# Laying a column of scores over the partitions: TensorE transposes in place of f32 products with the unit matrix

## The chip, the cores and the metric

The kernel runs on one core of one Trainium2 chip. The metric is the device time of one execution in microseconds (us), taken as the median of several runs. TensorE does the matrix products, ScalarE (ACT in the profile) and VectorE (DVE) the elementwise work, GpSimd (POOL) and SyncE (SP) small work and most of the DMA issues.

## The reference, cut to what matters

Four graph layers run one after the other on 1250 nodes with 1024 features and 20000 edges; each normalises its input, applies ReLU, computes, and adds to the residual.

- Layer 0 takes `x1 = h @ W1 + b1` (512 features) and then applies four gates. A gate is, per edge, `alpha = tanh(x_i @ gw[:512] + x_j @ gw[512:] + gb)` with `i` the receiver and `j` the sender; each node gets the sum over its edges of `norm * alpha * x_j`.
- Layer 1 is a product with a sparse 1024x1024 matrix, plus a bias. Layer 2 is a graph convolution: a product with W and a sum over neighbours.
- Layer 3 is graph attention: `al = h @ a_l`, `ar = h @ a_r`, `e = exp(-leaky_relu(al[src] + ar[dst]))`, and each node gets the sum of `e * h[dst]` over its edges divided by the sum of `e`, through an ELU.

In both the gates and the attention a score of one node of an edge meets a score of the other node. The kernel treats the graph as a dense matrix of edge counts, so it needs one score along the partitions and the other along the free dimension, the same on every partition.

## The kernel before, in words

The 1250 nodes are padded to 1280, ten tiles (`T`) of 128 rows (`P`); `HT` is five tiles. Every engine runs its own list of instructions in an order written out by hand; semaphores join them. f32 values that go into a product are split into a high and a low part (`_hi`, `_lo`, type fp32r), and a product is three matmuls: hi by hi, hi by lo, lo by hi.

**Gates.** A gate has two halves of receivers (five tiles each), so there are eight halves, `q` 0 to 7. `half_pe(q, r, h)` walks over the ten tiles `s` of senders. For each `s` it does 15 matmuls, five receiver tiles `dd` by three (lines 2482 to 2484), with a block of the mask as the stationary operand and `g_hi` or `g_lo` as the moving one. The mask of a tile `s` is made ahead of it: ACT takes `tanh(U_ALL + v[:, s])` (line 1306), DVE multiplies by the edge counts (line 1841), ACT rounds it to `mask_hi` (line 1311), DVE takes the rest as `mask_lo` (line 1846). The masks lie in a ring of five. DVE reads the finished sums (`take_sums`, line 1856), takes the next scores `u` and `v` by two dot products per tile (`gates`, lines 1716 and 1719), and the low part `g_lo` (line 1724) of what ACT has rounded (`g_hi`, line 1294).

`U_ALL` is 640 columns of PSUM that hold, on every partition, the scores `u` of the five receiver tiles of a half. `spread_u(q, h)` fills it. It waits for the scores (`u_ready`) and until ACT has read the old values for the last time (`tanh_ready`), and does five f32 matmuls whose stationary operand is one column of `u` repeated 128 times (an access pattern of stride 0) and whose moving operand is the unit matrix `ident`. The spread for `q` + 1 is issued in half `q` before tile `s` = 7; the one for `q` = 0 stands in the last tile of the product before the gates (`x1_pe`, `t` = 9, `k` = 2). That makes eight calls, 40 products. ACT's first tanh of a half and one of DVE's `gates` wait for it.

**Attention.** The product of layer 3 is `turned_product(dense[2], ...)`; its matmuls are line 758, and transposes of whole tiles are line 741. DVE takes `al` and `ar` per tile (lines 2150, 2153, 2159). `spread_al` lays `al` over the partitions in the same way, into `TRANSPOSED`: eight tiles (`AL_FIRST`) in the middle of the product of the last tile (`k` = 4), the two others in the first group of the aggregation before `s` = 5. ACT copies the result to `al_all` (lines 1570 and 1554), and ACT and DVE make the attention matrix from it (lines 1519, 2167, 1510, 2171, 1525, 2176); `gat_step` (line 2602) is the aggregation, with the same three matmuls, one group of two receiver tiles after another.

Between the gates and the product of layer 1 lies a chain with transfers: a tile of x is stored, loaded, normalised, its squares are written out (`squares_of_rows`) and read back turned (`turned`), and its parts `hT_hi` (line 652) and `hT_lo` (line 658) feed line 758.

Other places use TensorE's transpose already: line 741 (f32, tiles of the input), line 2346 (f32, rows of weights) and line 2355 (bf16).

Of the kernel before, what the change touches and what calls it, by code (L numbers as in the profile page):

```python
# [24 lines left out]
P = 128  # L25
# [30 lines left out]
HT = T // 2  # L56
# [51 lines left out]
def build_program(nc, x, src, dst, edge_weight, w1, b1, gate_w, gate_b, bias1, w2, b2, w3_dram, att, out):  # L108
# [13 lines left out]
    def small(name, shape, dtype):  # L122
        size = 4 if dtype in (F32, F32R, I32) else 2
        for n in shape[1:]:
            size *= n
        offset = places[0]
        places[0] = -(-(offset + size) // 32) * 32
        assert places[0] <= limit, name
        return at(name, shape, dtype, offset)
# [175 lines left out]
    ident = small("ident", [P, P], F32)  # L305
# [26 lines left out]
    u = small("u", [P, T], F32)  # L332
    v = small("v", [P, T], F32)
    al = small("al", [P, T], F32)
# [196 lines left out]
    TRANSPOSED = ps[:, 6 * BANK:8 * BANK]  # L531
# [16 lines left out]
    U_ALL = ps[:, HT * BANK:HT * BANK + HALF]  # L548
# [1730 lines left out]
    def _(pe):  # L2279
# [88 lines left out]
        def spread_u(q, h):  # L2368


            pe.wait_ge(u_ready, HT * q + HT)
            pe.wait_ge(tanh_ready, 2 * HT * q)
            for dd in range(HT):
                last = nc.tensor.matmul(U_ALL[:, dd * P:(dd + 1) * P], u[:, h * HT + dd:h * HT + dd + 1].to_broadcast([P, P]), ident[:, :],
                                        start=True, stop=True)
            last.then_inc(u_spread, 1)

        def open_bank(b):
# [3 lines left out]
        def x1_pe(t):  # L2382

            b = t % 2
            pe.wait_ge(hT_lo_ready, t + 1)
            if t == 1:
                pe.wait_ge(blend_chain, 3)
                open_bank(1)
            if t + 1 < T and t + 1 != LATE_TILE:
                transpose_pe(pe, d0, (t + 1) // 2, (t + 1) % 2)  # L2390
            for k in range(KT):
                if t + 1 == LATE_TILE and k == KT // 2:
                    transpose_pe(pe, d0, LATE_TILE // 2, LATE_TILE % 2)
                if k % 2 == 0:
                    place_pe(t, k // 2)
                if k == 0:
                    pe.wait_ge(bias_placed, t + 1)
                if t == 1 and k == KT // 2:
                    sum_captured()
                if t == T - 1 and k == 2:  # L2400
                    pe.wait_ge(product_read[0], HT)
                    spread_u(0, 0)
                if t == 0:
                    pe.wait_ge(w_lo_ready, k + 1)
                nc.tensor.matmul(PRODUCT0[b], hT_hi[b][:, k, :], w1_hi[:, k, :], start=False, stop=False, skip_group_check=True)  # L2405
                nc.tensor.matmul(PRODUCT0[b], hT_hi[b][:, k, :], w1_lo[:, k, :], start=False, stop=False, skip_group_check=True)  # L2406
                last = nc.tensor.matmul(PRODUCT0[b], hT_lo[b][:, k, :], w1_hi[:, k, :], start=False, stop=(k == KT - 1), skip_group_check=True)  # L2407
            last.then_inc(product_ready[b], 1)
# [11 lines left out]
        with pe.If(whole == 0):  # L2420
# [4 lines left out]
            with pe.Fori(0, T) as a:  # L2425
# [6 lines left out]
                with pe.Fori(0, GENERAL_CHUNKS) as c:  # L2432
                    n = a * GENERAL_CHUNKS + c
                    pe.wait_ge(gen_ready, n + 1)
                    for q in range(CHUNKS):
                        columns = onehot[q]
                        for lo, hi in BLOCKS:
                            last = nc.tensor.matmul(COUNTS[:, lo:hi], dsel[0:EP, 0, q, :], columns[0:EP, lo:hi], start=False, stop=False, skip_group_check=True)
                        for half, (lo, hi) in zip(WEIGHTS, weight_blocks):
                            for k in range(3):  # L2440
                                last = nc.tensor.matmul(half, dsel[0:EP, 1 + k, q, :], columns[0:EP, lo:hi], start=False, stop=False, skip_group_check=True)
# [3 lines left out]
                for half, (lo, hi) in zip(WEIGHTS, weight_blocks):  # L2445
                    last = nc.tensor.matmul(half, zeros[:, :], iota_h[:, lo:hi], start=False, stop=True, skip_group_check=True)
                last.then_inc(gen_summed, 1)
                pe.wait_ge(gen_copied, 2 * a + 2)
                for s in range(T):
                    last = nc.tensor.transpose(COUNT_T[:, s * P:(s + 1) * P], count_f[:, s * P:(s + 1) * P], ident[:, :])  # L2450
# [12 lines left out]
        def half_pe(q, r, h):  # L2463

            for s in range(T):
                k = s % SLOTS
                if s == HT + 2 and not is_last(q):
                    spread_u(q + 1, 1 - h)
                if s == T - 1 and is_last(q):
                    pe.wait_ge(tanh_ready, 2 * GATES * T)  # L2470
                    transpose_pe(pe, dense[1], 0, 0)
                if h == 0:
                    pe.wait_ge(g_lo_ready, T * r + s + 1)
                pe.wait_ge(mask_lo_ready, 2 * HT * q + s + 1)
                order = LAST_SUMS if is_last(q) and s == T - 1 else range(HT)
                for n, dd in enumerate(order):
                    if is_first(q) and s == 0 and dd == HT - 1:
                        pe.wait_ge(product_read[1], HT)
                    if s == 0 and not is_first(q):
                        pe.wait_ge(sum_read, HT * q - HT + dd + 1)  # L2480
                    cols = slice(dd * P, (dd + 1) * P)
                    nc.tensor.matmul(SUMS[dd], mask_hi[k][:, cols], g_hi[:, s, :], start=(s == 0), stop=False)  # L2482
                    nc.tensor.matmul(SUMS[dd], mask_hi[k][:, cols], g_lo[:, s, :], start=False, stop=False)  # L2483
                    last = nc.tensor.matmul(SUMS[dd], mask_lo[k][:, cols], g_hi[:, s, :], start=False, stop=(s == T - 1))  # L2484
                    if s == T - 1 and n < HT - 1:
                        last.then_inc(sum_ready, 1)
                last.then_inc(mask_used, 1)
# [98 lines left out]
        def spread_al(tiles):  # L2586

            pe.wait_ge(al_copied, tiles[-1] + 1)
            for t in tiles:
                last = nc.tensor.matmul(TRANSPOSED[:, (t - tiles[0]) * P:(t - tiles[0] + 1) * P],  # L2590
                                        al[:, t:t + 1].to_broadcast([P, P]), ident[:, :], start=True, stop=True)
            last.then_inc(al_spread, 1)

        turned_product(dense[2], lambda b: pe.wait_ge(unit_read, (UNIT_OF["S4", 3] + 1, UNIT_OF["A22", 2] + 1)[b]), lambda: spread_al(range(AL_FIRST)))

        def gat_step(s, j, ns):
# [10 lines left out]
        def quarter_step(s, q):  # L2607

            cols = slice(P, 2 * P)
            of = slice(HID + q * QUARTER, HID + (q + 1) * QUARTER)  # L2610
            for left, rights in ((att_hi[s][:, cols], (y_hi[s], y_lo[s])), (att_lo[s][:, cols], (y_hi[s],))):
                for right in rights:
                    last = nc.tensor.matmul(LAST_QUARTERS[q], left, right[:, of], start=(s == 0 and len(rights) == 2 and right is y_hi[s]),
                                            stop=(s == T - 1 and len(rights) == 1))
            return last
# [5 lines left out]
        def gat_pe(grp, first):  # L2621

            for s in range(T):
                if first:
                    pe.wait_ge(product_read[s % 2], dense[2].pairs(s // 2 + 1))
                    if s == HT:
                        pe.wait_ge(al_all_ready, 1)
                        spread_al(range(AL_FIRST, T))
                pe.wait_ge(att_lo_ready, T * grp + s + 1)
                for j in range(GRP):  # L2630
                    if s == 0 and not first:
                        pe.wait_ge(gat_read, GRP * grp - GRP + j + 1)
                    last = gat_step(s, j, range(2))
                    if j == GRP - 1:
                        last.then_inc(att_used, 1)
                    if s == T - 1:
                        row_sums(j).then_inc(gat_ready, 1)
# [18 lines left out]
        for q in range(2):  # L2656
            for s in range(T):
                last = quarter_step(s, q)
# [24 lines left out]
```

## Time and profile before

| | before |
|---|---|
| median of 3 runs | 967.32 us (967.18 to 970.75) |
| the profiled execution, its own time | 967.41 us |
| its span, first to last instruction | 965.6 us |
| TensorE busy | 943.4 us, 98% |
| VectorE, ScalarE, GpSimd busy | 705.7, 495.2, 154.4 us |
| mean granted TensorE clock | 0.996 |

PE is TensorE's matmuls and PEld its loads of the stationary operand, which run beside them. Starts of instructions are measured; the ends of matmuls are modelled, so the cost of a matmul in a dense stream is read from one start to the next, not from its duration. "Idle before" with a name behind an arrow is the time for which an engine waited, and for what.

### The profile page before, as it was taken

The numbers are of one execution on the slowest core, as the hardware profiler recorded it, in microseconds if no ns is written. First come the engines' busy times: TensorE is split into PE (matmuls) and PEld (weight loads), VectorE is DVE, ScalarE is ACT, GpSimd is POOL, SyncE is SP. The second block draws the span as 40 slices with busy tenths as digits, with TensorE's granted clock in tenths as the row PEclk, the third lists the DMA queues.
The fourth block names the chain that finished last, engine by engine and source line by source line (L and its number), as shares of the span: only waits on it lengthen the run. The fifth ranks groups of instructions, "written<-read, shape, count | busy, mean of one in ns | idle before, by whom it ended". The sixth has DMA issues, their size and how long they took to land.

```text
span 965.6 us, 13857 instructions
## 1 busy us (share of the span) xinstructions
PE 943.4 (98%) x5011; PEld 783.1 (81%) x5012; DVE 705.7 (73%) x1243; ACT 495.2 (51%) x759; POOL 154.4 (16%) x247
## 2 busy tenths in 40 slices
PE   5999999999999999979999999999999999999998
PEld 3888878888888888868888888888888888888887
DVE  7887797797788788638763244598757875967787
ACT  5788874554554557324433453443623223656654
POOL 3023410000000001213342000013320000333331
PEclk9999999999999999999999999999999999999999
DMA  7256492000000005299982400042986532201222
GB/s 260 89 195 232 118 205 85 0 23 1 0 22 0 0 0 119 48 286 295 315 241 109 161 1 2 1 55 89 229 192 210 170 113 82 88 25 62 88 87 82
DMA packets 41433, 105.75 MB, mean 110 GB/s; under 512 B 6136, under 2 KB 14524, under 8 KB 41232
## 3 DMA queue, kind: packets, MB, share of 16 engines
q1 hardware_dynamic: 29056, 70.27, 21.6%
q0 software_dynamic: 12320, 34.74, 15.8%
q8 instruction: 34, 0.56, 0.3%
q14 instruction: 23, 0.19, 0.1%
HBM read 63.03 MB, written 47.20 MB: 114 GB/s over the span
## 4 chain that ended last, share of the span: by engine, by line
PE 90%; DVE 4%; DMA 3%; ACT 2%; issue 1%; POOL 1%; SPq 0%; DVEq 0%; ACTq 0%; POOLq 0%
PE ps L758 21%; PE ps L2602 14%; PE ps L2577 10%; PE ps L2482 9%; PE ps L2484 8%; PE ps L2483 8%; PE ps L2550 5%; PE ps L2546 5%; PE ps L2405 2%; PE ps L2407 2%; PE ps L2406 2%; PE ps L741 1%; DMA squares_of_rows<-squares 1%; DVE wt_lo L588 1%; PE ps L2330 1%; PE ps L2333 1%
## 5 line engine op out<-in xcount | busy, mean ns | idle before, releaser
L2482 PE MATMUL ps<-g_hi,mask_hi 128*128 128x512 f32 x400 | 157.6, 394 | 0.2 <-DVE mask_lo L1846 0.2
L2484 PE MATMUL ps<-g_hi,mask_lo 128*128 128x512 f32 x400 | 155.9, 390 | 0.0
L2483 PE MATMUL ps<-g_lo,mask_hi 128*128 128x512 f32 x400 | 155.8, 389 | 0.0
L1306 ACT ACTIVATE mask<-ps,v 128x640 f32<-128x640 f32 x80 | 63.1, 793 | 95.7 <-PE ps L2484 49.1
L2602 PE MATMUL ps<-y_all,att_hi 128*128 128x512 f32 x380 | 103.6, 392 | 0.0
L2482 PEld LDWEIGHTS ps<-g_hi,mask_hi 128*128 128x128 f32 x400 | 75.1, 188 | 19.1 <-DVE mask_lo L1846 2.3
L2484 PEld LDWEIGHTS ps<-g_hi,mask_lo 128*128 128x128 f32 x400 | 75.1, 188 | 15.9
L2483 PEld LDWEIGHTS ps<-g_lo,mask_hi 128*128 128x128 f32 x400 | 75.1, 188 | 14.9
L2577 PE MATMUL ps<-w_hi,parts 128*128 128x512 f32 x280 | 86.5, 389 | 0.0
L758 PE MATMUL ps<-w,hT_hi 128*128 128x512 f32 x320 | 85.8, 390 | 0.0
L2602 PEld LDWEIGHTS ps<-y_all,att_hi 128*128 128x128 f32 x380 | 70.4, 188 | 14.8 <-issue 0.4
L717 ACT ACTIVATE xin<-xin,shift 128x1024 f32<-128x1024 f32 x30 | 34.4, 1148 | 81.0 <-DVE shift L600 81.0
L1841 DVE TENSOR_TENSOR mask<-mask,countT 128x640 f32<-128x640 f32 x80 | 65.4, 819 | 14.0 <-ACT mask L1306 13.9
L1311 ACT ACTIVATE mask_hi<-mask 128x640 fp32r<-128x640 f32 x80 | 59.0, 737 | 28.4 <-DVE mask L1841 27.9
L758 PE MATMUL ps<-wt_hi,hT_hi 128*128 128x512 f32 x160 | 63.6, 397 | 6.6 <-DVE hT_lo L658 6.6
L758 PEld LDWEIGHTS ps<-w,hT_hi 128*128 128x128 f32 x320 | 59.8, 188 | 12.5
L1846 DVE TENSOR_TENSOR mask_lo<-mask,mask_hi 128x640 fp32r<-128x640 f32 x80 | 65.1, 818 | 1.2 <-ACT mask_hi L1311 1.2
L2550 PE MATMUL ps<-cnt,hs 128*128 128x512 f32 (+1 forms) x240 | 64.8, 351 | 0.0
L2546 PE MATMUL ps<-cnt,hs 128*128 128x512 f32 (+1 forms) x240 | 64.6, 351 | 0.0
L758 PE MATMUL ps<-wt_lo,hT_hi 128*128 128x512 f32 x160 | 63.1, 394 | 0.0
L2577 PEld LDWEIGHTS ps<-w_hi,parts 128*128 128x128 f32 x280 | 52.6, 188 | 10.8
L2602 PE MATMUL ps<-y_all,att_lo 128*128 128x512 f32 x190 | 59.4, 390 | 0.0
(255 smaller groups left out, 1952.3 us busy)
## 6 DMA issues: line engine op xcount, KB each, us to landing
xin<-x_after SPq DMA_DIRECT2D x20, 512.0 KB, 5.4
squares_of_rows<-squares SPq DMA_DIRECT2D x16, 512.0 KB, 4.1
turned<-squares_of_rows SPq DMA_DIRECT2D x64, 128.0 KB, 2.9
x_after<-g POOLq DMA_DIRECT2D x20, 256.0 KB, 7.6
x_after<-row_all POOLq DMA_DIRECT2D x10, 512.0 KB, 8.4
xres<-x_after POOLq DMA_DIRECT2D x10, 512.0 KB, 5.7
x_after<-xres POOLq DMA_DIRECT2D x10, 512.0 KB, 4.7
xin<-in_x SPq DMA_DIRECT2D x9, 512.0 KB, 3.7
```

What stands on the lines that cost most here:

```text
L758: last = nc.tensor.matmul(PRODUCT[d.n][b][:, half * BANK:(half + 1) * BANK], left[:, k, :], right[k][:, half * BANK:(half + 1) * BANK], st ...
L1306: nc.scalar.activation(mask[k][:, :], U_ALL, ACT.Tanh, bias=v[:, s:s + 1]).then_inc(tanh_ready, 1)
L1311: nc.scalar.activation(mask_hi[k][:, :], mask[k][:, :], ACT.Copy).then_inc(mask_hi_ready, 1)
L1841: nc.vector.tensor_tensor(mask[k][:, :], mask[k][:, :], countT[:, s, h * HALF:(h + 1) * HALF], ALU.mult).then_inc(mask_ready, 1)
L1846: nc.vector.tensor_tensor(mask_lo[k][:, :], mask[k][:, :], mask_hi[k][:, :].bitcast(F32), ALU.subtract).then_inc(mask_lo_ready, 1)
L2482: nc.tensor.matmul(SUMS[dd], mask_hi[k][:, cols], g_hi[:, s, :], start=(s == 0), stop=False)
L2483: nc.tensor.matmul(SUMS[dd], mask_hi[k][:, cols], g_lo[:, s, :], start=False, stop=False)
L2484: last = nc.tensor.matmul(SUMS[dd], mask_lo[k][:, cols], g_hi[:, s, :], start=False, stop=(s == T - 1))
L2546: nc.tensor.matmul(sums[j], hs[:, f, s, 0, j * P:(j + 1) * P], columns, start=(s == 0), stop=False)
L2550: last = nc.tensor.matmul(sums[j], hs[:, f, s, 1, j * P:(j + 1) * P], columns, start=False, stop=(s == T - 1))
L2577: last = nc.tensor.matmul(UNIT_BANK[n], left, right[:, k, :], start=(kind != "A22" and k == 0 and len(rights) == 2 and right is W2_HI[w]), ...
L2602: last = nc.tensor.matmul(AGG[j][:, n * BANK:(n + 1) * BANK], left, right[:, n * BANK:(n + 1) * BANK], start=(s == 0 and len(rights) == 2 ...
```

## The change

The products of `spread_u` and `spread_al` become transposes of the same operand, the stride-0 column, against the same `ident`. The destination, the order, the waits and the semaphores stay as they are; no other line is touched.

```diff
             for dd in range(HT):
-                last = nc.tensor.matmul(U_ALL[:, dd * P:(dd + 1) * P], u[:, h * HT + dd:h * HT + dd + 1].to_broadcast([P, P]), ident[:, :],
-                                        start=True, stop=True)
+                last = nc.tensor.transpose(U_ALL[:, dd * P:(dd + 1) * P], u[:, h * HT + dd:h * HT + dd + 1].to_broadcast([P, P]), ident[:, :])
             last.then_inc(u_spread, 1)
...
             for t in tiles:
-                last = nc.tensor.matmul(TRANSPOSED[:, (t - tiles[0]) * P:(t - tiles[0] + 1) * P],
-                                        al[:, t:t + 1].to_broadcast([P, P]), ident[:, :], start=True, stop=True)
+                last = nc.tensor.transpose(TRANSPOSED[:, (t - tiles[0]) * P:(t - tiles[0] + 1) * P],
+                                           al[:, t:t + 1].to_broadcast([P, P]), ident[:, :])
             last.then_inc(al_spread, 1)
```

## Rows read from the trace of the kernel before

**Rows 1.** The page: busy time and share; the chain's shares; one DMA (us to landing).

```profile
PE 943.4 (98%) x5011; PEld 783.1 (81%) x5012; DVE 705.7 (73%) x1243; ACT 495.2 (51%) x759; POOL 154.4 (16%) x247
...
PE 90%; DVE 4%; DMA 3%; ACT 2%; issue 1%; POOL 1%; SPq 0%; DVEq 0%; ACTq 0%; POOLq 0%
...
squares_of_rows<-squares SPq DMA_DIRECT2D x16, 512.0 KB, 4.1
```

**Rows 2.** Waits of PE: us in total, times, longest us.

```profile
PE ps L758 <- DVE hT_lo L658: 6.6, 1, 6.6
...
PE ps L2482 <- DVE mask_lo L1846: 0.2, 1, 0.2
```

**Rows 3.** The lines asked for: duration ns min/median/max, first and last start.

```profile
L2374 PEld LDWEIGHTS ps<-ident,u x80: 187/190/192, 116.5 to 359.3; 128*128 128x128 f32 x80
L2374 PE MATMUL ps<-ident,u x80: 271/275/275, 116.7 to 359.4; 128*128 128x128 f32 x80
...
L741 PEld LDWEIGHTS ps<-ident,xin x112: 138/140/231, 7.7 to 716.7; 128*128 128x128 f32 x112
L741 PE MATMUL ps<-ident,xin x112: 270/273/476, 7.7 to 716.8; 128*128 128x128 f32 x112
```

**Rows 4.** PE in order of time: start us, us, instruction; five products in a gate.

```profile
146.61 1.28 PE L2374 MATMUL ps<-ident,u 128*128 128x128 f32 x10
147.65 0.47 PE L2482 MATMUL ps<-g_hi,mask_hi 128*128 128x512 f32 x1
```

**Rows 5.** The same view: eight products, then two, in layer 3.

```profile
814.88 1.95 PE L2590 MATMUL ps<-ident,al 128*128 128x128 f32 x16
816.58 1.17 PE L758 MATMUL ps<-w,hT_hi 128*128 128x512 f32 x4
...
836.04 0.61 PE L2590 MATMUL ps<-ident,al 128*128 128x128 f32 x4
836.40 1.18 PE L2602 MATMUL ps<-y_all,att_hi 128*128 128x512 f32 x4
```

**Rows 6.** The same view: eight transposes inside the last half, and eight of weights.

```profile
400.96 1.03 PE L741 MATMUL ps<-ident,xin 128*128 128x128 f32 x8
401.75 0.48 PE L2482 MATMUL ps<-g_hi,mask_hi 128*128 128x512 f32 x1
...
84.03 1.03 PE L741 MATMUL ps<-ident,xin 128*128 128x128 f32 x8
84.90 0.20 PE L2330 MATMUL ps<-right,left 125*128 125x90 bf16 x1
```

**Rows 7.** ACT, DVE and PE in order of time, first tiles of half 0.

```profile
118.03 0.80 ACT L1306 ACTIVATE mask<-ps,v 128x640 f32<-128x640 f32 x1 [0.16 <-PE ps L2374]
...
128.11 0.82 DVE L1846 TENSOR_TENSOR mask_lo<-mask,mask_hi 128x640 fp32r<-128x640 f32 x1
...
131.65 0.81 DVE L1846 TENSOR_TENSOR mask_lo<-mask,mask_hi 128x640 fp32r<-128x640 f32 x1
...
128.53 0.39 PE L2484 MATMUL ps<-g_hi,mask_lo 128*128 128x512 f32 x1
129.08 0.47 PE L2482 MATMUL ps<-g_hi,mask_hi 128*128 128x512 f32 x1 [0.15 <-DVE mask_lo L1846]
```

**Rows 8.** ACT, DVE and PE in order of time, end of half 1.

```profile
183.18 0.79 ACT L1306 ACTIVATE mask<-ps,v 128x640 f32<-128x640 f32 x1 [4.31 <-PE ps L2374]
...
184.62 0.75 DVE L1724 SCALAR_TENSOR_TENSOR g_lo<-g,dis,g_hi 128x512 fp32r<-128x512 f32 x1 [5.79 <-ACT g_hi L1294]
...
191.09 3.38 DVE L1856 SCALAR_TENSOR_TENSOR g<-ps,dis,g 128x512 f32<-128x512 f32 x5
...
182.81 0.47 PE L2482 MATMUL ps<-g_hi,mask_hi 128*128 128x512 f32 x1
...
193.16 0.39 PE L2482 MATMUL ps<-g_hi,mask_hi 128*128 128x512 f32 x1
```

**Rows 9.** Busy us (instructions) of PE, PEld, DVE, ACT, POOL, clock, DMA share, GB/s.

```profile
182.00:217.00 35.00, 35.00 (x160) 28.68 (x159) 31.03 (x54) 19.87 (x28) 0.00 (x0) 1.00 0.04 16
362.00:405.00 43.00, 42.95 (x193) 35.06 (x192) 32.20 (x45) 24.74 (x31) 5.29 (x6) 1.00 0.33 80
```

**Rows 10.** The chain that ended last, between the gates and layer 1's second tile.

```profile
408.56 1.21 DVE stats L596 x2
...
412.79 11.03 DMA squares_of_rows<-squares
...
425.20 7.20 DMA turned<-squares_of_rows
...
434.87 1.21 PE ps L758 x2
```

**Rows 11.** As rows 9: the clock before, in and after TensorE's longest pause.

```profile
400.00:410.00 10.00, 10.00 (x49) 8.09 (x49) 6.53 (x14) 2.51 (x3) 5.30 (x7) 1.00 0.69 110
430.00:435.00 5.00, 0.13 (x1) 0.14 (x1) 1.49 (x2) 2.09 (x2) 0.00 (x0) 0.73 1.07 361
435.00:440.00 5.00, 5.00 (x14) 3.96 (x15) 3.60 (x6) 1.15 (x1) 0.57 (x1) 0.59 1.06 253
```

**Rows 12.** ACT, DVE and PE in order of time after the spread of `al`.

```profile
816.86 1.03 ACT L1570 ACTIVATE al_all<-ps 128x1024 f32<-128x1024 f32 x1 [4.59 <-PE ps L2590]
...
829.92 0.42 DVE L2176 TENSOR_TENSOR att_lo<-att_e,att_hi 128x256 fp32r<-128x256 f32 x1
...
833.16 0.41 DVE L2176 TENSOR_TENSOR att_lo<-att_e,att_hi 128x256 fp32r<-128x256 f32 x1
...
830.48 1.16 PE L2602 MATMUL ps<-y_all,att_hi 128*128 128x512 f32 x4
```

## The prediction

> **What bounds the kernel now.** I read the page first: TensorE is busy for 943.4 of 965.6 us and carries 90% of the chain that ended last, VectorE 4%, DMA 3% [rows 1]. So a microsecond taken out of TensorE's stream is worth a microsecond, unless something else is waiting just behind it. PE's waits show where that is: 6.6 us in one piece for `hT_lo` of layer 1, and 0.2 us for one `mask_lo`; in between PE does not stand still [rows 2]. Then I looked at the changed lines themselves, and read neighbouring starts from the timeline, because ends of matmuls are modelled: the cost of a spread is the time from its first start to the start of what follows.
>
> **What the change removes and adds.** The 40 products of `spread_u` leave 80 records, so an f32 product is two of them; a transpose on line 741 leaves one (112 records are 14 calls of eight) [rows 3]. The durations, 275 and 273 ns, are alike and say nothing; starts do. Ten records of product take 147.65 - 146.61 = 1.04 us [rows 4], sixteen take 1.70, four take 0.36 [rows 5]: a slope of (1.70 - 0.36) / 12 = 0.112 us a record and an offset of -0.09. Eight transposes in the same surroundings, a dense stream of 512-column matmuls, take 401.75 - 400.96 = 0.79 us [rows 6]; the line for products gives 8 x 0.112 - 0.09 = 0.81 for eight records. So a transpose costs what half an f32 product costs, and I price it as one record:
>
> - five instead of ten records: 1.04 - (0.56 - 0.09) = 0.57 us for a call of `spread_u`;
> - eight in place of sixteen: 1.70 - 0.79 = 0.91 us;
> - two in place of four: 2 x 0.112 = 0.22 us.
>
> From the other side: eight transposes before narrow bf16 matmuls took 0.87 us, 0.109 each [rows 6]. At that price with no offset the savings are 0.50, 0.83 and 0.14.
>
> What the trace does not show is a transpose of a stride-0 column. The row that is nearest says the repetition is free in a plain load: the stationary load of `u` takes 190 ns. The load of a transpose takes 140 ns at full stride [rows 3]. I take 140, or anything that stays hidden. Bounds: the longest transpose of the trace, 476 ns [rows 3], which would make a transpose dearer than the two records it replaces; and no cost beyond the 0.10 us of its start to start.
>
> A rule of the Trainium skill differs from the row. "TensorE: Matmul & The Clock Gate", section Terms, says that transpose mode is four times faster for FP32. The trace shows a factor of 0.224 / 0.10, about two, and the sum goes by the trace; by that rule a spread of five would take 1.12 / 4 = 0.28 us and the kernel would come out near 960 us (it returns as a rival below).
>
> **Which savings reach the end.** Taking the ten calls in order of time:
>
> - *The first `spread_u`, before half 0: nothing.* PE starts the third tile of half 0 at 129.08, 0.55 us after the start before it where 0.23 is usual, because `mask_lo` ran from 128.11 to 128.93 [rows 7]. In those first tiles DVE has two mask passes, one `g_lo` and two dot products per tile: 131.65 - 128.11 = 3.54 us from one `mask_lo` to the next [rows 7], to PE's 15 matmuls at (193.16 - 182.81) / 45 = 0.23 [rows 8], 3.45. DVE and ACT got there by a chain that starts in the edge counts and the tables, and that does not pass through the spread except for one tanh that had waited 0.16 us [rows 7]. PE will finish the spread 0.57 us earlier and wait that much longer for the mask. If I am wrong the kernel gains 0.57 more.
> - *The seven others: 7 x 0.57 = 4.0 us.* PE does not wait at all from there to the last half. The danger is that DVE is nearly as busy: 31.0 of 35 us in half 1 [rows 9]. But DVE's late part of that half is released by the spread itself: ACT waited 4.31 us for line 2374, its first tanh started at 183.18, its `g_hi` followed, and DVE, which had stood idle for 5.79 us, went on at 184.62 and reached the sums at 191.09 [rows 8]. PE's first matmul of the next half, which needs the first of those sums read, starts at 193.16, 2 us after that. A spread that ends 0.57 us earlier moves ACT and DVE forward by the same 0.57. The shorter half still leaves DVE 34.4 - 31.0 = 3.4 us.
> - *The pause between gates and layer 1 neither gives nor takes.* Its chain starts behind the gates: DVE's statistics at 408.56, a store of squares that takes 11.03 us, their way back 7.20 us [rows 10]. The DMA engines are full there but were a third full from 362 to 405 [rows 9], so the queue is made by work that follows PE, and moves with it.
> - *The spreads of `al`: 0.91 + 0.22 = 1.1 us.* ACT waited 4.59 us for the first, then 13 us of attention work on ACT and DVE lead to the `att_lo` that ends at 830.34 and lets PE start at 830.48 [rows 12]. Natural would have been about 830.3, so the two chains are level here. Both of them start at the end of the spread, so both come 0.91 us earlier. At the second PE has slack: the `att_lo` of the tile that follows it started at 833.16 and PE took it up at 836.40 [rows 5, 12].
>
> No DMA, wait or semaphore is added or moved; SP's and POOL's queues keep their order. PE gets 50 records and 50 loads fewer.
>
> **The sum.** 4.0 + 0.9 + 0.2 = 5.2 us with roundings (7 x 0.575 = 4.03, 0.91, 0.22). The profiled execution took 967.41 us around its span of 965.6, and lies 0.1 above the median of the three. 967.4 - 5.2 = 962.2 us, a gain of 0.53%. The bounds: 7 x 0.50 + 0.83 + 0.14 = 4.5 us by the dearer transpose, 5.2 + 0.57 = 5.8 with the first spread counted. One more thing moves the result: in the pause the granted clock fell to 0.5, the 1.2 GHz level, for about 1.35 / 0.5 = 2.7 us of 430 to 435 and 4.1 us of 435 to 440 [rows 11]; PE worked again from 434.87 [rows 10] and the clock rose at about 439.1, so (439.1 - 434.87) / 2 = 2.1 us are lost. In another execution that could be nothing, or all 6.8 us could fall on work and cost 3.4. So the forecast's own range is 960.4 to 963.8.
>
> **The rivals.**
>
> - *Transposes as forecast: 962.2 us. 0.70.*
> - *The change does nothing on TensorE:* for a repeated column the transpose costs the same 0.22 us as a product, two passes under another name. For it: no row shows this operand in a transpose. Against: line 741 has one record where a product has two [rows 3]. 967.4 us. 0.07.
> - *Half of it is eaten by the pause:* the transfers behind 412.79 run on a clock of their own, PE reaches the pause 4.0 us sooner and waits 10.6 instead of 6.6. For it: an 11 us store where the page's median is 4.1 [rows 1, 10], so the engines are contended. Against: the low share before 405 [rows 9]. Only the spreads of `al` remain: 967.4 - 1.1 = 966.3 us. 0.08.
> - *Transposes at a quarter of a product:* the saving per transpose would be 0.224 - 0.056 = 0.17 us, times 45 (7 x 5 + 8 + 2) 7.6 us: 959.8 us. Against: 0.79 us for eight [rows 6]. The rule of the Trainium skill named above says this. 0.06.
> - *The other side, a slow load:* the stationary load of a repeated column in transpose form reads one address 128 times and blocks PE. At 0.224 us a transpose nothing is won, and at 0.224 + 4.84 / 45 = 0.33 us the kernel is 0.5% slower; at the 0.476 us of the longest transpose [rows 3] it loses 45 x 0.25 = 11 us: 979 us. Against: 190 ns for the plain load of this column, no more than any other f32 load. 0.04.
> - *The clock falls:* transposes do not hold the full clock, and every run of five brings a fall like that in the pause, worth up to 3.4 us [rows 11]; two falls outweigh the gain, nine calls would cost 30 us: some 990 us. Against: 400 to 410, with eight transposes in it, has clock 1.00 [rows 11]. "TensorE: Matmul & The Clock Gate", section Part 4: PE-mode transpose, of the Trainium skill says that transposes do not count as busy for the clock; by that rule this would be likelier than I make it. 0.03.
> - Something else: 0.02.
>
> **How the numbers follow.** The time is that of the likeliest, 962.2 us. From 959.8 to 966.6 the range takes in nearly all of the forecast's own (0.65), the quarter price and the pause: 0.79, about 8 in 10; no change and the slow cases lie above it. About 0.5%, or 4.84 us, is what a measurement of this kernel can tell from no change: that is 962.48, and my forecast lies just beyond it. Of the forecast's 0.70 I give 0.41 to faster; with the quarter price and a little of the rest faster is 0.49. Within 0.5% are 0.29 of the forecast, no change, the pause and a little of the slow cases: 0.46. Slower 0.05.
>
> **What the profile after would show.** Line 2374 and its twin should have 40 and 10 records in place of 80 and 20, with a load near 140 ns. The start after a spread of five should follow at about 0.47 us, after eight at 0.79. The wait for `mask_lo` at the third tile of half 0 should grow by about half a us. The last half should begin 4.0 us sooner, the wait for `hT_lo` should stay near 6.6, and the end of the spread of `al` should be 4.9 us sooner. If the spacing is 0.22 the product was never the cost; if the wait for `hT_lo` has grown the pause took it. The prediction fails by little if the clock falls for another stretch than before, and by much only if a repeated column loads slowly.

## The result and the profile after

The changed kernel takes 960.43 us in the median of five runs (959.77 to 962.06), the kernel before 967.32 (967.17 to 970.75). The ratio is 0.9929, with a 95% interval of 0.9916 to 0.9943. The forecast was 962.2 us, a gain of 5.2; measured are 6.9. The profiled execution took 961.20 us with a span of 959.5.

The spreads in the profile after: duration ns min/median/max for the first line of the group, then PE in order of time.

```profile
L2374 PEld LDWEIGHTS ps<-ident,u x40: 134/136/137, 115.2 to 354.0; 128*128 128x128 f32 x40
L2374 PE MATMUL ps<-ident,u x40: 271/272/273, 115.4 to 354.1; 128*128 128x128 f32 x40
...
115.42 0.71 PE L2374 MATMUL ps<-ident,u 128*128 128x128 f32 x5
...
179.90 0.71 PE L2374 MATMUL ps<-ident,u 128*128 128x128 f32 x5
180.37 0.48 PE L2481 MATMUL ps<-g_hi,mask_hi 128*128 128x512 f32 x1
...
809.88 1.03 PE L2589 MATMUL ps<-ident,al 128*128 128x128 f32 x8
810.67 1.17 PE L758 MATMUL ps<-w,hT_hi 128*128 128x512 f32 x4
...
830.10 0.38 PE L2589 MATMUL ps<-ident,al 128*128 128x128 f32 x2
830.24 1.17 PE L2601 MATMUL ps<-y_all,att_hi 128*128 128x512 f32 x4
```

Half of the records are left, and from one start to the next a spread takes 0.47 us where it took 1.04 [rows 4], 0.79 for 1.70 and 0.14 for 0.36 [rows 5]. The durations of a record, 272 for 275 ns, still say nothing. The load of the repeated column takes 136 ns, no more than the 140 of a column that is not repeated [rows 3].

The waits of PE and the places where it starts after one:

```profile
PE ps L758 <- DVE hT_lo L658: 7.5, 1, 7.5
...
PE ps L2295 <- POOL ew_part L1011: 1.3, 1, 1.3
PE ps L2481 <- DVE mask_lo L1846: 0.4, 1, 0.4
...
119.86 0.39 PE L2406 MATMUL ps<-w_hi,hT_lo 128*128 128x512 f32 x1
120.33 0.47 PE L2481 MATMUL ps<-g_hi,mask_hi 128*128 128x512 f32 x1
...
127.78 0.47 PE L2481 MATMUL ps<-g_hi,mask_hi 128*128 128x512 f32 x1 [0.39 <-DVE mask_lo L1846]
...
422.36 0.61 PE L758 MATMUL ps<-wt_hi,hT_lo 128*128 128x512 f32 x2
430.43 0.79 PE L758 MATMUL ps<-wt_hi,hT_hi 128*128 128x512 f32 x1 [7.46 <-DVE hT_lo L658]
```

With landmarks in both profiles the 6.1 us between the two spans can be laid out. The kernel before has its last start ahead of the pause at 427.69; the other numbers stand in the rows here, in [rows 4, 5, 7, 10] and in the two spans.

| stretch | before | after | difference |
|---|---|---|---|
| start of the program to the first spread | 116.72 | 115.42 | -1.30 |
| first spread to the third tile of half 0 | 12.36 | 12.36 | 0.00 |
| third tile to the last start ahead of the pause | 298.61 | 294.58 | -4.03 |
| over the pause | 7.18 | 8.07 | +0.89 |
| end of the pause to the spread of `al` | 380.01 | 379.45 | -0.56 |
| spread of `al` to the end | 150.72 | 149.62 | -1.10 |

Three rows are the change: 0.00, 4.03 and 1.10. Three are not in its code: the start, the pause, and the stretch behind the pause, where PE runs at half speed for a while, about 3 us here and about 4 before. The second row of the change can be seen in each half. PE from one spread to the next, first the kernel before (its earlier spread is in [rows 4]), then the changed one:

```profile
181.77 1.28 PE L2374 MATMUL ps<-ident,u 128*128 128x128 f32 x10
```

```profile
145.32 0.71 PE L2374 MATMUL ps<-ident,u 128*128 128x128 f32 x5
```

That is 181.77 - 146.61 = 35.16 us before and 179.90 - 145.32 = 34.58 after, 0.58 less; the halves that follow save 0.57 to 0.61 each. ACT, DVE and the next half follow the spread as they did before:

```profile
180.74 0.80 ACT L1306 ACTIVATE mask<-ps,v 128x640 f32<-128x640 f32 x1 [3.74 <-PE ps L2374]
...
182.18 0.75 DVE L1724 SCALAR_TENSOR_TENSOR g_lo<-g,dis,g_hi 128x512 fp32r<-128x512 f32 x1 [5.22 <-ACT g_hi L1294]
...
188.64 2.06 DVE L1856 SCALAR_TENSOR_TENSOR g<-ps,dis,g 128x512 f32<-128x512 f32 x3
...
190.69 0.39 PE L2481 MATMUL ps<-g_hi,mask_hi 128*128 128x512 f32 x1
```

DVE's first sum stands 2.05 us ahead of PE's start of the next half, 2.07 before [rows 8]: the spread carries DVE with it. ACT and DVE waited 0.57 us less each.

### The profile page after: what moved, and what is told of

Same layout as the page of the kernel before. It is cut to its first block, busy times and chain, and to the rows that moved or that the text cites. A ratio compares the mean times of both kernels' runs of the same rounds, so it can differ in the third digit from the quotient of the medians.

```text
span 959.5 us, 13757 instructions
## 1 busy us (share of the span) xinstructions
PE 936.8 (98%) x4961; PEld 776.0 (81%) x4962; DVE 705.5 (74%) x1243; ACT 494.9 (52%) x759; POOL 155.4 (16%) x247
## 4 chain that ended last, share of the span: by engine, by line
PE 89%; DVE 5%; DMA 3%; ACT 2%; issue 1%; SPq 0%; DVEq 0%; ACTq 0%
PE ps L758 21%; PE ps L2601 14%; PE ps L2576 10%; PE ps L2481 9%; PE ps L2483 8%; PE ps L2482 8%; PE ps L2549 5%; PE ps L2545 5%; PE ps L2404 1%; DMA xin<-in_x 1%; PE ps L2406 1%; PE ps L2405 1%; DMA squares_of_rows<-squares 1%; PE ps L741 1%; DVE wt_lo L588 1%; PE ps L2330 1%
```

## The experiments

The theory to be tested: the gain is the number of TensorE records times 0.112 us, the first spread excepted. Rivals: the pause eats a part; the change makes the start of the program faster, or wins in some way that is not the number of records. "Gain" is the difference of medians on the same chip; the ratio goes with its interval.

**Only the spreads of u.** The edit is the first hunk of the diff alone.

> Only the spreads of u are transposes; the spreads of al stay f32 products. Price theory (a record is worth 0.112 us, the first spread nothing): 7 x 0.57 = 4.0 us faster, ratio 0.9958. Rival, the pause between gates and layer 1 eats what comes before it: under 1 us faster, and the wait for hT_lo near 10.6 us. Rival, the change shortens the start of the program as well (the changed kernel reached the first spread 1.3 us sooner): 5.3 us faster and the first spread near 115.4 us.

963.74 us, ratio 0.9961 (0.9947 to 0.9976), a gain of 3.4 us by the medians and 3.8 by the ratio, near the price theory's 4.0. The wait for `hT_lo` was 6.1 us, not 10.6, and the first spread started at 117.86, 1.1 us later than in the kernel before. Both rivals fail here.

**Only the spreads of al.** The second hunk alone.

> Only the spreads of al are transposes. Price theory: 1.1 us faster, ratio 0.9988, all of it behind 814 us. Rival, a saving of 1 us here is lost because the attention chain on ACT and DVE is level with PE: no difference, and a longer wait for att_lo at the fourth tile. Rival of the start: 2.4 us faster.

965.88 us, ratio 0.9985 (0.9976 to 0.9995): 1.2 to 1.5 us for the 1.1 expected. From the spread (815.03) to the end of the span (964.7) it is 149.67 us, as in the changed kernel.

**The kernel before, once more,** without an edit.

> The kernel before, unchanged. All theories: ratio 1.000. It shows how far the profiled start of the program differs from execution to execution: if the 1.3 us by which the changed kernel reached its first spread sooner is chance, this profile can have its first spread anywhere from about 115 to 117 us; if it belongs to the change, at 116.7.

966.93 us, ratio 0.9996 (0.9987 to 1.0005). Its profile has the first spread at 115.07, so the 1.3 us at the start are chance. In the profiles of this study that start lay between 115.07 and 117.86 us, whatever the kernel. Two things vary there. One is how long PE waits for `ew_part` behind the first loads, 0.6 to 3.6 us. The other is how long PE then still runs at half speed, 0.43 us from start to start: to 22.57 us in the first profile of the kernel before, and only to about 19.9 in this one. Both had waited 2.0 us for `ew_part`, and yet their first spreads are 1.65 us apart.

The stretches of the table tell the change from chance. The three rows of the change add up to 461.69 us in the first profile of the kernel before and to 461.74 in this one. In the changed kernel they are 456.56 us, and 456.57 in its second profile (below). That is 5.1 to 5.2 us both times. The three other rows add up to anything from 502.8 to 505.1 us in the eleven profiles without a filled pause, with transposes or with products.

**Every transpose twice.**

```diff
-            for dd in range(HT):
+            for dd in [dd for _ in range(2) for dd in range(HT)]:
...
-            for t in tiles:
+            for t in [t for _ in range(2) for t in tiles]:
```

> Every transpose of both spreads is issued twice, so that PE makes as many records as before the change. Price theory (a transpose costs what half an f32 product costs): ratio to before 1.000, within 0.5 us, starts after a spread of ten 1.04 us later. Rival, the change wins in another way than by the number of records (start, or ACT getting the scores earlier): still 1 us or more faster than before. Each record of a transpose being dearer than one of a product, 0.120 against 0.112: 0.4 us slower.

966.88 us, ratio 0.9993 (0.9983 to 1.0003). With as many records as before the gain is gone, within the interval. PE in order of time in this kernel:

```profile
181.36 1.25 PE L2374 MATMUL ps<-ident,u 128*128 128x128 f32 x10
182.37 0.48 PE L2481 MATMUL ps<-g_hi,mask_hi 128*128 128x512 f32 x1
```

Ten transposes take 1.01 us, ten records of product 1.04 [rows 4]: a transpose is a little cheaper than half a product, not dearer. Nothing else of the change shows a weight of its own.

**The changed kernel again.**

> The changed kernel once more, beside others on one chip. Price theory, now with only_u at 0.9961 and only_al at 0.9985: the parts add up to 5.2 us, ratio 0.9946. The first comparison gave 0.9929 (6.9 us); if a part of that belongs to the change as a whole and to neither part alone, it comes again: ratio 0.993.

961.12 us, ratio 0.9938 (0.9925 to 0.9951), a gain of 6.3 us by the medians. The sum of the parts, 0.9946, lies inside the interval, and so does the first comparison's 0.9929. The wait for `hT_lo` was 6.5 us this time.

**All but the first spread.**

```diff
             for dd in range(HT):
-                last = nc.tensor.transpose(U_ALL[:, dd * P:(dd + 1) * P], ...)
+                if isinstance(q, int) and q == 0:
+                    last = nc.tensor.matmul(U_ALL[:, dd * P:(dd + 1) * P], ..., start=True, stop=True)
+                else:
+                    last = nc.tensor.transpose(U_ALL[:, dd * P:(dd + 1) * P], ...)
```

> As the changed kernel, but the spread before half 0 stays a product. Theory that the first spread is worth nothing since PE waits for the mask anyhow: the same time as the changed kernel, and a wait for mask_lo at the third tile back at 0.15 us (a step from start to start of 0.55 in place of 0.78). Rival, every spread is worth its 0.57 us: 0.6 us slower than the changed kernel.

963.15 us, ratio 0.9951 (0.9939 to 0.9964). The medians are 2 us apart and the intervals overlap, so the time alone can't settle half a microsecond. The profile can. In order of time, PE:

```profile
116.88 1.28 PE L2375 MATMUL ps<-ident,u 128*128 128x128 f32 x10
...
128.69 0.39 PE L2487 MATMUL ps<-g_hi,mask_lo 128*128 128x512 f32 x1
129.24 0.47 PE L2485 MATMUL ps<-g_hi,mask_hi 128*128 128x512 f32 x1 [0.16 <-DVE mask_lo L1846]
```

From the first spread to the third tile it is 129.24 - 116.88 = 12.36 us, the same as in the changed kernel (127.78 - 115.42) and in the kernel before (129.08 - 116.72, [rows 7] and the table above). The wait stands at 0.16 with the product and at 0.39 with the transpose. The first spread is worth nothing up to there.

**Every product twice.** The same loops as above, in the kernel before.

> The kernel before, with every product of both spreads issued twice: 80 and 20 more records. Price theory: 7 x 10 x 0.112 + 20 x 0.112 = 10.1 us slower, and up to 1.1 more for the first spread, since its wait covers at most 0.57 us or so of the 1.12: 10.1 to 11.2 us, ratio 1.0105 to 1.0115. Rival, PE has slack and absorbs it, or ACT and DVE fall behind for lack of scores: clearly less, or more than 12 us.

977.81 us, ratio 1.0102 (1.0088 to 1.0117): 10.4 us slower by the medians, 9.9 by the ratio. Behind the spread of `al` (824.54) it is 977.5 - 824.54 = 152.96 us, 2.24 more than before, which is 20 x 0.112. From the first spread (116.56) to the third tile (130.01) it is 13.45 us, 1.09 more: making the first spread longer costs nearly all of its 1.12, though making it shorter gains nothing. ACT's first tanh then waits 1.28 us for the spread, where it had waited 0.16 [rows 7], and the mask comes late with it. From the third tile to the pause it is 7.89 us more. By the stretches the cost is thus 7.89 + 2.24 + 1.09 = 11.2 us, where the medians say 10.4; the interval, 8.5 to 11.3 us, holds both.

**A transpose at full stride.**

```diff
-                last = nc.tensor.transpose(U_ALL[:, dd * P:(dd + 1) * P], u[:, h * HT + dd:h * HT + dd + 1].to_broadcast([P, P]), ident[:, :])
+                last = nc.tensor.transpose(U_ALL[:, dd * P:(dd + 1) * P], ident[:, :], ident[:, :])
```

> As the changed kernel, but the spread of u transposes the unit matrix itself, 128 columns side by side, in place of one column repeated: the gates then get other scores and the output is not the reference's. If the repetition of the column costs or saves nothing: the same time as the changed kernel, five transposes 0.46 to 0.47 us, the load 138 to 140 ns in place of 136. If it slows the load: this kernel is faster than the changed one.

962.13 us, ratio 0.9942 (0.9928 to 0.9956), as the changed kernel. The load, in ns:

```profile
L2374 PEld LDWEIGHTS ps<-ident x40: 138/140/143, 115.6 to 354.4; 128*128 128x128 f32 x40
```

140 against 136: repeating a column costs nothing, the load even takes 4 ns less.

**The pause filled, in the changed kernel and in the one before.** The clock behind the pause was the one place left where a microsecond could hide, so I took the fall of the clock away.

```diff
             free(1)
+            if d.n == 1:
+                for _ in range(24):
+                    nc.tensor.matmul(PRODUCT[1][1][:, 0:BANK], zeros[:, :], zeros[:, 0:1].to_broadcast([P, BANK]), start=True, stop=True, skip_group_check=True)
             product_pe(pe, d, 0, 1, False, None)
```

> The changed kernel with 24 products of zeros, 512 columns each, put into TensorE's pause before the second tile of layer 1 (24 x 0.227 = 5.4 us of a pause of 7 to 8; their bank is overwritten by the product that follows). The step from one start to the next after the pause showed half speed for 3 to 5.5 us in each profile, 1.5 to 3 us lost. If the clock then stays at full speed: 1.5 to 3 us faster than the changed kernel, near 959 us, ratio to before 0.991. Rival, the products of zeros do not hold the clock, or the chain of transfers behind the pause gets longer: the same time as the changed kernel or slower.

> The kernel before with the same 24 products of zeros in the pause. It tells whether the 1 us by which the change beat the sum of its parts (6.0 to 6.9 against 5.2 us) lies in the clock after the pause. If it does: this kernel is 2.1 to 3 us faster than before, ratio 0.9975, and the distance to the changed kernel with the pause filled is 5.2 us. If the extra belongs elsewhere the distance is 6 us or more.

The changed kernel with it: 960.24 us, ratio 0.9926 (0.9910 to 0.9942). The kernel before with it: 965.02 us, ratio 0.9985 (0.9973 to 0.9996), a gain of 2.0 us. Busy us, clock (third from the end), DMA share and GB/s, first of the changed kernel, then of the changed kernel with the pause filled:

```profile
425.00:430.00 5.00, 0.00 (x0) 0.00 (x0) 0.93 (x1) 2.02 (x2) 0.00 (x0) 0.67 1.06 355
430.00:435.00 5.00, 4.57 (x14) 3.67 (x15) 3.60 (x7) 1.22 (x2) 0.57 (x1) 0.65 0.98 249
```

```profile
425.00:430.00 5.00, 4.66 (x21) 3.53 (x19) 0.05 (x1) 1.06 (x2) 0.04 (x1) 1.00 1.06 341
430.00:435.00 5.00, 3.61 (x16) 3.00 (x17) 3.57 (x6) 2.19 (x2) 0.57 (x1) 1.00 1.04 262
```

Products of zeros hold the clock at its 2.4 GHz level. In the kernel before that is worth 2.0 us by the medians and 1.5 by the ratio, for the 2.1 us which the prediction had read as lost. The two profiles agree: from the end of the pause to the spread of `al` it is 378.03 us with the pause filled, 380.01 without. The two filled kernels are 4.8 us apart by their medians, and 0.9926 / 0.9985 = 0.9941 gives 5.7: on either side of 5.2. The pair shows no gain of 6 us or more, but with intervals of 1 to 1.5 us each it can't place a missing one either.

**The changed kernel a third time.**

> The changed kernel a third time. Sum of the parts: ratio 0.9946. If the first two comparisons (0.9929 and 0.9938) were not chance: 0.993 to 0.994 again.

961.87 us, ratio 0.9945 (0.9927 to 0.9962): the sum of the parts. The profiled execution was an odd one of 967.81 us. It shows something that I had not looked for. DVE, then PE, in order of time:

```profile
156.83 0.15 DVE L1865 COPY gb_col<-gb 128x1 f32 x1 [5.86 <-DMA gw<-in_L_gnn_gate_w]
...
158.46 3.38 DVE L1856 SCALAR_TENSOR_TENSOR g<-ps,dis,g 128x512 f32<-128x512 f32 x5
...
156.33 0.39 PE L2483 MATMUL ps<-g_hi,mask_lo 128*128 128x512 f32 x1
159.26 0.50 PE L2481 MATMUL ps<-g_hi,mask_hi 128*128 128x512 f32 x1 [2.54 <-DVE g L1856]
...
161.12 0.63 PE L2482 MATMUL ps<-g_lo,mask_hi 128*128 128x512 f32 x1
161.55 0.63 PE L2483 MATMUL ps<-g_hi,mask_lo 128*128 128x512 f32 x1
```

The weights of the second gate (`gw`, 512 KB) are loaded while the DMA engines are full (a busy share of 0.83 to 1.22 from 138 to 150 us in this profile); in this execution the transfer took 18.37 us in the chain that ended last, and 12.7 in the first profile of the changed kernel. DVE waits for it at the head of half 1, ahead of two mask passes and the sums for which PE waits next. PE stood for 2.54 us and then, from 161.1 to 164.1, ran at half speed, 0.43 us from start to start, with a granted clock of 0.50. From its second spread to its third it is 39.03 us in place of 34.58: 4.45 us of the 6.7 by which this span is longer than that of the profile before it (966.1 for 959.4). Another 2.1 us lie behind the pause, with a wait of 0.87 us at line 2549 for which the profile names no cause.

The filled kernel's profile has the same event in a smaller form: a transfer of 16.3 us, a wait of 3.79 us on DVE, then 0.47 us of PE for `g` and 0.37 for `mask_lo`, and 36.05 us from the second spread to the third. That is 1.47 us more than usual, with the clock at 1.00 behind the waits.

**DVE's wait moved to the first use of gw.** On top of the filled pause:

```diff
             if nxt is not None:
-                dve.wait_ge(gw_landed, 16 * (nxt + 1))
                 if h == 1:
...
                     if s == 1:
+                        dve.wait_ge(gw_landed, 16 * (nxt + 1))
                         dve.wait_ge(sum_read, HT * q)
```

> The changed kernel with the pause filled, and with DVE's wait for the gate's weights (gw) moved from the head of half 1 to its first use, behind two mask passes and the five sums. In the profiles so far DVE stood in that wait for 0.5 to 5.9 us at the head of half 1, and in the longest case PE then waited 2.5 us for the sums and ran at half speed behind that. If this is what the late wait costs: no PE wait for g or mask_lo near 158 us in the profile even when gw lands late, a median as in the filled kernel (960.2) or up to 0.5 us below, and no execution several us above the others. Rival, the late transfer was not the cause: executions of 964 us and more as before.

960.29 us, ratio 0.9935 (0.9920 to 0.9951), runs from 959.11 to 962.76. In its profile DVE waits for no transfer in half 1, though `gw` took 14.3 us and landed about 1.4 us after DVE had passed the old place of the wait; from the second spread to the third it is 34.58 us. But in the changed kernel's second profile a wait of 1.83 us at the old place had cost nothing either, and no execution of this kernel is known to have had `gw` later than that. So the wait as the cause of the lost 4.45 and 1.47 us is read from the rows of two profiles, and the move of the wait is not shown to bring them back. The median is no better than with the pause filled alone.

## Why the prediction was right

- **The price of a transpose** was taken as one record, 0.112 us. Five take 0.47 us (0.47 forecast), eight 0.79 (0.79), two 0.14 (0.36 - 0.22 = 0.14). Doubling the transposes gave back the time of before (0.9993), doubling the products cost 9.9 to 10.4 us (8.5 to 11.3 by the interval) where the price, with the first spread's 1.09 counted, gives 11.2.
- **The repeated column,** the one unknown, costs nothing: 136 ns for the load, 140 at full stride. The slow load as a rival is out, and so is "no change on TensorE".
- **Seven spreads on the path: 4.0 us.** The profile has 4.03, and 3.90 between the second profiles of the two kernels, with DVE carried along by the spread as reasoned; the spreads of u alone brought 3.4 to 3.8.
- **The first spread: nothing.** 12.36 us to the third tile in all three kernels (before, changed, all but the first). A detail was off: I placed the whole wait at the third tile. 0.24 us of it fell at the first (0.47 from start to start where 0.23 is usual) and 0.23 at the third; the step just behind the first wait, 0.30, holds most of the rest.
- **The pause neither gives nor takes.** The wait for `hT_lo` was 6.6 before and 7.5, 6.5 and 6.7 in three profiles of the changed kernel, 6.1 with only the spreads of u: it varies by about a microsecond and does not follow from PE's earlier arrival.
- **The spreads of al: 1.1 us.** 1.10 in the profile, 1.2 to 1.5 by themselves.
- **The clock.** No fall beside any spread: in the 3 to 4 us around each of the ten the granted clock of the changed kernel is 1.00, and its mean is 0.996 as before. The rule that transposes don't count as busy for the clock, from the Trainium skill, "TensorE: Matmul & The Clock Gate", section Part 4: PE-mode transpose, changes nothing here, where a spread is 0.5 us inside a dense stream; no run here shows a long stretch of nothing but transposes. Nor did the four times of that page's section Terms come true: the factor is 1.04 / 0.47, about two.
- **The range** of 960.4 to 963.8 us does not follow from its own terms: 967.4 - 5.8 - 2.1 gives 959.5, and 967.4 - 4.5 + 1.3 (the 3.4 us of a fall wholly on work less the 2.1 already lost) gives 964.2. The measured 960.43 lies at the very edge of the stated range and well inside the worked one.
- **The path.** One danger was not in the prediction: a late `gw` holds up DVE in half 1, and by the rows that cost 1.47 and 4.45 us in two of the fourteen profiled executions. The forecast of DVE's slack held in the others.

Too small was the total: 5.2 us forecast, and 6.9, 6.3 and 5.1 by the medians of three comparisons. No term is mis-sized by the profiles, and the parts measured alone add up to 0.9961 x 0.9985 = 0.9946, 5.2 us, though with intervals of 1.4 and 0.9 us either way. In the first pair of profiles the difference beyond the change is the start (1.30), the pause (-0.89) and the clock behind it (0.56), and the start and the stretch behind the pause differ as much between two profiles of the unchanged kernel (1.65 and 0.79 us; its pauses by 0.41). Those three stretches add up to 502.9 and 502.8 us in the first two profiles of the changed kernel, the two lowest of eleven; its third had 505.1, and the other kernels with transposes 503.2 to 505.1. So in the profiles the change is 5.1 to 5.2 us and the rest is luck. For the executions without a profile, from which the medians come, that is inferred. The interval of the first comparison ends at 0.9943 and just misses 0.9946; the two later ones hold it.

## What to carry to other kernels

Price a TensorE edit by the records and by the step from start to start in the surroundings where it will stand; modelled durations of a product and of a transpose were the same here although one costs twice the other. Laying a column over the partitions in f32 was cheaper here as a transpose of the repeated column than as a product with the unit matrix, half the time from start to start, and each such spread counted in full only where TensorE was not about to wait for someone else. When a measured gain is larger than the sum, run the kernel before once more with a profile before giving the excess a cause.

## What the runs showed that I had not expected

- A spread ahead of a wait is lopsided: 0.57 us shorter gained 0.00, 1.12 us longer cost 1.09, since it also starts the chain that ends the wait (ACT waited 1.28 us for it).
- TensorE's pause of 7 to 8 us costs more than itself: filling it with 24 products of zeros kept the granted clock at 1.00 and took 2.0 us off the kernel before by the medians (0.4 to 2.6 by the interval). Of the changed kernel's versions the filled one had the lowest median beside it, 960.24 against 961.87, with intervals that overlap.
- A load of 512 KB, issued while the DMA engines were full, landed late enough in one execution to hold PE for 2.54 us, with the clock down behind it. DVE waited for that load in eight of the fourteen profiles. Up to 1.8 us of waiting cost nothing; with 3.8 us the half was 1.5 us longer, and with 5.9 us 4.45.
